# A causal second-order linear attention with a top-2 expert layer on one core: VectorE's order of work inside a batch, and the order in which the next batch's q and k are made

## The reference

```python
q, k, v = (split into 16 heads of 16)(xn @ Wq.T, xn @ Wk.T, xn @ Wv.T)
qf, kf = taylor_exp(q), taylor_exp(k)        # [1, x/2, (x outer x)/sqrt(2)/4]
A = tril(qf @ kf.T)                          # per head, 512 x 512
y = (A @ v) / (sum over m <= n of A + EPS)
attention = y.reshape(512, 256) @ Wo.T

logits = xn @ Wg                             # 8 experts
top_w, top_i = top_k(logits, 2); top_w = softmax(top_w)
expert_e(x) = (silu(x @ W1[e]) * (x @ W2[e])) @ W3[e]     # 256 -> 512 -> 256
experts = sum over the two chosen experts of top_w * expert(xn)
```

## Time and profile before

| | us |
|---|---|
| median of 2 runs | 688.08 |
| lowest, highest | 687.91, 688.25 |
| profiled execution | 690.13 |
| its span | 688.4 |
| TensorE busy / weight loads | 643.7 / 494.4 |
| VectorE / ScalarE / GpSimd busy | 411.1 / 342.6 / 346.5 |
| mean granted TensorE clock | 0.983 of full speed |

### The profile page before, as it was taken

The page is one execution under the profiler, slowest core; times in us unless marked ns, Lnnn a source line. Parts: engine busy times, 40 slices in busy tenths (PEclk is TensorE's granted clock), DMA queues, the critical chain, the costliest instruction groups (busy, mean ns, idle before and its releaser), DMA issues.

```text
span 688.4 us, 16296 instructions
## 1 busy us (share of the span) xinstructions
PE 643.7 (94%) x5351; PEld 494.4 (72%) x5351; DVE 411.1 (60%) x1067; ACT 342.6 (50%) x515; POOL 346.5 (50%) x381
## 2 busy tenths in 40 slices
PE   8889999989898999987999999999999999999994
PEld 7455665656665665644788888888888888888884
DVE  6766776877687665685785444545454545444442
ACT  3568777677778676764563232323232232323231
POOL 3264654637363635465145555555555555545442
PEclk9899999999999999997999999999999999999998
DMA  3644454545444443553743333333333333333332
GB/s 128 139 115 106 113 148 114 152 114 123 117 105 98 105 107 95 148 160 130 244 107 49 63 64 50 63 53 60 64 58 55 64 49 64 49 64 51 62 44 27
DMA packets 37773, 64.05 MB, mean 93 GB/s; under 512 B 8288, under 2 KB 25824, under 8 KB 37696
## 3 DMA queue, kind: packets, MB, share of 16 engines
q0 software_dynamic: 16704, 28.12, 20.9%
q1 hardware_dynamic: 20432, 34.24, 20.3%
q10 hardware_dynamic: 560, 0.66, 0.3%
HBM read 27.72 MB, written 22.68 MB: 73 GB/s over the span
## 4 chain that ended last, share of the span: by engine, by line
PE 72%; DVE 11%; issue 5%; DMA 5%; ACT 3%; SPq 2%; POOL 1%; POOLq 0%; DVEq 0%
PE banks L1172 27%; PE banks L1193 14%; PE banks L1052 8%; PE banks L1034 5%; PE banks L1072 4%; PE banks L1181 4%; PE banks L1116 3%; DVE Q L747 3%; DMA out<-yo,xw 2%; PE banks L1161 2%; ACT Q L556 2%; PE banks L1081 2%; DVE yw L722 1%; PE banks L1107 1%; SPq L307 1%
## 5 line engine op out<-in xcount | busy, mean ns | idle before, releaser
L503 POOL DMA_INDIRECT out<-yo,xw x71 | 114.1, 1607 | 159.3 <-DVE yo L992 85.7
L476 POOL TENSOR_SCALAR_AFFINE_SELECT T<-T 128x512 f32<-128x512 f32 x128 | 79.8, 635 | 121.1 <-ACT T L528 51.7
L628 ACT ACTIVATE sTh<-banks 128x512 fp32r<-128x512 f32 x71 | 42.5, 598 | 195.4 <-PE banks L1181 195.4
L1172 PE MATMUL banks<-w12h,xgh 128*128 x284 | 118.8, 418 | 2.5 <-DVE xa L782 1.7
L984 DVE TENSOR_TENSOR sTl<-banks,sTh 128x512 fp32r<-128x512 f32 x71 | 49.0, 690 | 108.9 <-ACT sTh L628 108.7
L1172 PE MATMUL banks<-w12l,xgh 128*128 x284 | 112.6, 397 | 0.0
L1172 PE MATMUL banks<-w12h,xgl 128*128 x284 | 112.6, 396 | 0.0
L492 POOL DMA_INDIRECT xg<-xs_scr,glist x71 | 71.1, 1001 | 24.2 <-issue 23.0
L1052 PE MATMUL banks<-T,vau 128*17 128x512 f32 (+3 forms) x1024 | 77.2, 442 | 2.3 <-POOL T L476 2.3
L1034 PE MATMUL banks<-Q,K 32*128 32x256 f32 (+2 forms) x1024 | 71.7, 363 | 5.9 <-DMA Q<-Q 2.9
L467 POOL DMA_INDIRECT xs_scr<-xb,slots x64 | 67.2, 1050 | 18.4 <-issue 9.6
(11 more groups left out here) (172 smaller groups left out, 1215.2 us busy)
## 6 DMA issues: line engine op xcount, KB each, us to landing
Q<-Q SPq DMA_DIRECT2D x128, 64.0 KB, 2.4
w12r<-w SPq DMA_DIRECT2D x16, 512.0 KB, 4.3
out<-xa SPq DMA_DIRECT2D x16, 256.0 KB, 2.4
w3r<-w SPq DMA_DIRECT2D x8, 512.0 KB, 5.1
K<-Kt SPq DMA_DIRECT2D x124, 32.0 KB
xa<-x SPq DMA_DIRECT2D x7, 512.0 KB, 4.7
xg<-xs_scr,glist POOLq DMA_INDIRECT x71
out<-yo,xw POOLq DMA_INDIRECT x71, 3.8
```

Of the source, the lines that this page charges most:

```text
L476: e.affine_select(out=v, in_=v, pattern=[[0, 4], [1, P]], compare_op=ALU.is_ge, fill=-1.0, base=0, channel_multiplier=-1).then_inc(s["g_mk ...
L503: e.indirect_dma_start(out, bass.IndirectOffsetOnAxis(xw[:, t % 4, NE:NE + 1].bitcast(U32), 0), yo[:, t % 2, :], None, compute_op=ALU.add) ...
L1172: i = e.matmul(banks[:, 2 * (t % 2) + m, :], a[:, k, :], w[:, bass.ds(expert[t] * 4 + (2 * k + m), 1), :], start=(k == 0 and n == 0), stop ...
```

## The change

- In quarter 1, `place_rows(b)` moves from ahead of slot b (x's low parts, heads normalised) to behind it.
- In quarters 0 and 2 of all batches but the last, VectorE handles the other steps of slot b (T, and t: heads normalised) ahead of the c step. TensorE's and ScalarE's order doesn't change here.
- The next batch's first projections are swapped on all engines: q (c0) in quarter 1, k (c1) in quarter 2; `FIRST`, `made` and SyncE's moves follow.
- In quarter 2, `w12_low` moves from behind slot b to ahead of it, behind `variance`. The unit of the last batch stays where it was.
- `rsqrt(b + 2)` moves from the end of quarter 2 to quarter 3, behind `top(b + 1, 1)`.
- The eight sends of a batch come one mask later each; the eighth falls behind the first mask of the next batch's quarter 0. The last batch's own sends stay.

```diff
-        steps = [("c", b + 1, 0)]          # slot_b, quarter 2
+        steps = [("c", b + 1, 1)]
...
-    return ([("c", b + 1, 1)] if qd == 1 else []) + [("v", b + 1, 2 * qd - 2), ("v", b + 1, 2 * qd - 1)]
+    return ([("c", b + 1, 0)] if qd == 1 else []) + [("v", b + 1, 2 * qd - 2), ("v", b + 1, 2 * qd - 1)]
...
-    i = 3 * qd + min(m, 2) - (3 if b == LAST else 4)
+    k = 3 * qd + min(m, 2)
+    if k == 0:
+        return (b - 1, 7, 8) if b else None
+    i = k - (3 if b == LAST else 5)
...
-FIRST = (("x", 0, 0), ("x", 0, 1), ("c", 0, 1), ("c", 0, 0), *(("v", 0, i) for i in range(4)))
+FIRST = (("x", 0, 0), ("x", 0, 1), ("c", 0, 0), ("c", 0, 1), *(("v", 0, i) for i in range(4)))
...
-    return 4 * b + (2 - k if k < 2 else k + 1)
+    return 4 * b + k + 1
...
                     for h in range(2):
+                        move_q(e, b + 1, 0, h)
+                    for h in range(2):
                         move_k(e, b + 1, 0, h)
-                    for h in range(2):
-                        move_q(e, b + 1, 0, h)
...
                 elif qd == 1 and b < LAST:
                     places(b)
-                    place_rows(b)
-                elif qd == 2 and b < NBATCH - 2:
-                    variance(b + 2)
+                elif qd == 2:
+                    if b < NBATCH - 2:
+                        variance(b + 2)
+                    if (b, qd) in W12_LOW_WITH:
+                        w12_low(W12_LOW_WITH[b, qd])
                 elif qd == 3 and b < LAST:
                     top(b + 1, 1)
+                    if b < NBATCH - 2:
+                        rsqrt(b + 2)
...
-                if qd == 2 and (b, qd) in W12_LOW_WITH:
-                    w12_low(W12_LOW_WITH[b, qd])
+                elif qd == 1 and b < LAST:
+                    place_rows(b)
+                if n == NQ - 2:
+                    w12_low(8)
...
                     top(b + 1, 0)
-                    if b < NBATCH - 2:
-                        rsqrt(b + 2)
...
-                for item in slot_b(n):
+                items = slot_b(n)
+                if n % 4 in (0, 2) and n // 4 < LAST:
+                    items = [i for i in items if i[0] != "c"] + [i for i in items if i[0] == "c"]
+                for item in items:
                     step(*item)
```

More of the change, by code:

```diff
@@ L27 @@
 W12_WITH = {(1, 1): 0, (1, 2): 1, (2, 1): 2, (2, 2): 3, (3, 1): 4, (3, 2): 5, (4, 1): 6, (4, 2): 7, (7, 0): 8}
-W12_LOW_WITH = {(1, 2): 0, (1, 3): 1, (2, 2): 2, (2, 3): 3, (3, 2): 4, (3, 3): 5, (4, 2): 6, (4, 3): 7, (7, 2): 8}
+W12_LOW_WITH = {(1, 2): 0, (1, 3): 1, (2, 2): 2, (2, 3): 3, (3, 2): 4, (3, 3): 5, (4, 2): 6, (4, 3): 7}
 F32 = mybir.dt.float32
```

## The result

The changed kernel takes 671.88 us (median of 2 runs, 671.19 to 672.58) where the kernel before takes 688.08: a ratio of 0.9768 with a 95% interval of 0.9738 to 0.9798. So the gain is about 2%, and on which side of 2% it lies the runs do not agree.

The account below looks back on a forecast made before the run. TensorE, busy 222.3 of 240 us, was taken as the bound, its idle time as the possible gain. Terms 4.4 + 2.7 + 3.7 + 1.4 + 0.8 + 0.4 + 1.0 = 14.4 us gave 688.1 - 14.4 = 673.7; range 671 to 680.

Parts of the forecast that it names:

- Slots behind x's low parts: Quarter 1: x's low part and the projection's load come 0.74 us earlier; 4.4 us in batches 1 to 6.
- Swap of q and k: Batches 1 to 6: VectorE's wait for Kt is covered, so its loss counts nothing; batch 0 gains 1.0 us.
- Heads ahead of the low parts: Quarter 0, batches 1 to 6: heads normalised in VectorE's gap give TensorE 0.45 us each, 2.7 us together.
- Weight unit in a gap: Quarter 2, batches 1 to 4: unit in VectorE's idle gap removes yw's 0.92 us wait in quarter 3; 3.7 us.
- Rival 1: Quarter 2: VectorE reaches the unit 0.6 us later, GpSimd's select goes first; 5.5 us lost, 679.2; chance 0.12.
- Quarter 2: K's shorter low part replaces Q's; gain 0.18 us (batches 1 to 4), 0.33 (5 and 6), 1.4 together.
- Sends: Eighth send, in the next quarter 0, lands within 4.9 us; norm_x may slip to 178.6; no cost, 0.25 in hand.
- Rival 3: Eighth send late: each us of landing beyond 5.2 costs one in six batches; 679.7 (chance 0.10), slow form 701 (0.03).
- Batch 0: Start gains 0.8 us with first scores at 19.8; the second half's moves gain 0.4, the swap 1.0.
- Rivals 2: Wait moves to DMA (second half's moves) or ScalarE (quarter 0); 2.7 to 3.6 us lost, 677; chance 0.14.
- rival 4: ScalarE alone holds x's low parts, and the top-2 search refills yw's 0.92 us; 681.8; chance 0.05.
- The chances: Forecast (671 to 676.5) 0.56, rivals 0.44; within 2% 0.55, slower by over 2% 0.03; some 0.42 under 674.3.

Follow-up runs that it names:

- e1: Changed kernel with the slots' operations ahead of x's low parts again in quarter 1: ratio 0.9862 to the kernel before.
- e5: Changed kernel with the swap of q and k undone, all else changed: 687.27 us against 688.15 for the kernel before, ratio 0.9986.
- e12: Kernel before with only the swap of q and k: 681.86 us against 687.29, ratio 0.9911.
- e2: Changed kernel with the c step ahead of the heads again in quarters 0 and 2: ratio 0.986 to the kernel before.
- e8: Kernel before with only the weight unit of quarter 2 moved ahead of slot b: 685.19 us, ratio 0.9954.
- e3: Changed kernel with the weight unit of quarter 2 behind slot b again: ratio 0.9826 to the kernel before.
- e9: Changed kernel run again without an edit: 675.0 us, ratio 0.9822 to the kernel before.
- e4: Changed kernel with the eighth send one mask later still, behind the second mask of quarter 0: ratio 0.9808 to the kernel before.
- e7: Changed kernel with the eighth send two masks later, behind the last mask of quarter 0: 708.97 us, ratio 1.0305 to the kernel before.

## Why the prediction came out right, step by step

- **Slots behind x's low parts: right.** 0.74 predicted and 0.74 measured in quarter 1; undone 0.65 (e1). The rest of the load's wait is 0.73 where 0.64 was said.
- **Swap of q and k "costed at nothing" in batches 1 to 6: the step that failed**, though the sum hardly felt it. The prediction took the end of the Kt wait as covered, and saw its fall only as room for the slots. But the wait's end hangs on SyncE's queue, and the other parts move TensorE ahead of it. Undoing the swap gives back the whole gain (e5: 0.9986), and alone it gives 5.4 us (e12), partly the 3.7 that the prediction gave to the weight unit. That the sum came out is in part luck: the prediction let every quarter shrink without asking what a Kt wait that stayed would do: "without that cover up to 2.2 us a batch" was there and belonged beside each of the other terms, as the condition on which they hold. The Kt wait was the largest row, 17.5 us, and my reading of it stopped at what is late today.
- **Heads ahead of the low parts: the mechanism right, the size off.** 0.45 predicted, 0.60 measured (after, e2). The term was ScalarE's chain from K's high part to the squares. Its durations, 1.02 + 0.60, lead from 177.74 to 179.36 and to a gain of 0.37; the prediction wrote 179.28 and 0.45, a slip of 0.08. Its instructions start 0.91 and 0.48 apart, 0.23 less than the durations, and that gives the 0.60. The bound of 0.6 was VectorE's and held.
- **Weight unit in a gap: the 3.7 right as a sum, wrong as to whose it is.** Alone it gives 3.7 (e8), in the changed kernel nothing (e3), since the swap gives the same (e12). The unit took 1.22 as said. In the kernel before two selects began 0.11 ahead of it and it took 2.18; in e3 it began 0.01 ahead of a GpSimd instruction and that one was held up. The Trainium skill, "SBUF — State Buffer", section "Who interferes with whom", has it that the order of issue decides who waits; the traces agree in these two cases, while in e12, with the GpSimd instruction 0.63 ahead, neither was held up. Rival 1 did not come: VectorE reached the unit 1.1 us ahead of the select.
- **Quarter 2: 0.18 and 0.33 predicted, 0.31 measured** in the first profile, -0.1 to 0.3 in e9. This term lies within what executions of one kernel differ by.
- **Sends: no cost, as predicted, by a mechanism that was only half right.** From the send's start to `norm_x` it was 4.3 to 4.4 us in batches 3 and 4, inside the bounds of 2.9 and 4.9. `norm_x` did wait, 0.36 in batch 4, but its start 7.33 us into the quarter is where it was before (7.50). The room behind it is VectorE's 0.89 at x's low part a quarter later (e4), and not in quarter 0 where I looked for it. Rival 3's price of one us a us is borne out by e7 for the wait alone, with lost clock on top. Its limit was set too low: 8.0 us into the quarter by the prediction, where 8.16 cost nothing (e4) and the estimate from e4 and e7 is 8.9 to 9.2.
- **Batch 0.** First scores at 19.71, predicted 19.8, and by the chain that was predicted: K's moves (which ScalarE's queue issues here) start at 15.15, take 2.65, and the scores begin 1.91 behind. In e9 the same chain lies 1.2 us later as a whole. But the 0.8 won there went into a half clock that ended 1.7 us later, and quarter 0 gave 0.07 by its end. Quarter 1 gave 0.81 for 0.4 (the moves of the second half are not late at all), quarter 2 1.08 for 1.0.
- **Rivals 2 and 4** did not come: in batches 1 to 6 the scores of quarter 2 wait for no move, and e1 and e8 show both terms that rival 4 doubted to be real.
- **The chances.** 14.4 predicted; 15.6 in stage one of the profiled execution, 10.7 in e9's, and 12.3 between the medians of e9 and of the kernel before it. That "faster" and "same" had nearly equal chances was right: the two sets of runs fall one on either side of 2%.

## What to carry to other kernels

Moving work ahead pays only as long as nothing with a date of its own stands behind it (e5): before summing the gains of a quarter, look for the waits whose end is fixed by another queue (here sixteen moves of a buffer that has one copy), and take that gain back from the sum unless the same change removes them. When several edits aim at one wait, try each alone in the old kernel and take each out of the new one: here two edits each removed the same 3.7 us, and one of them could have been left out. Measure with a ruler inside the execution, such as the start of the same instruction in each stage; in quarters 0, 1 and 3 at full clock it told 0.1 us, where medians of 4 runs told 2 to 3 us. Look at the granted clock of each stretch first: e7's quarters 1 and e9's batch 7 were longer in part because the clock was halved.

## What the runs showed of the hardware

- Instructions that follow each other on ScalarE start before the recorded end of the one ahead: 1.02 long and 0.91 apart, 0.59 long and 0.48 apart. Sums of durations make a chain 0.1 us too long for each link.
- The granted clock was halved (1.2 for 2.4 GHz) for 6.8 us in batch 0 of each kernel without fillers, for 10.2 in e5. The fall came between 0.5 us ahead of the end of TensorE's wait of 2.7 to 2.9 us and 2.3 us behind it. In e7, where x's transposes stood 2.2 to 3.8 us in each of six batches, each of these quarters has such a stretch. In all fourteen traces every fall up to 345 us has a wait of TensorE (0.8 us or longer) beside it, still open or ended at most 2.3 us earlier, in e9's batch 7 one of only 1.2 to 1.3 us. The reverse does not hold: TensorE's six waits of 1.17 to 1.18 us in batches 1 to 6 of the kernel before brought no fall. What more it takes these runs don't tell.
- A GpSimd send that started during a late, long unit of the kernel before took 1.81 us instead of 0.98 (four times); with the unit moved ahead none of these four did.
- A send of 128 rows landed 2.9 (e4), 3.2 (e7) and 4.3 to 4.4 us (changed kernel) after its start. That is by `norm_x`, the instruction that waits for it, so each is an upper bound.
